# Three rounded products for the routing layer of a fused attention and slot-routing kernel

## The reference

```
x = x + attention(layernorm(x))
x = x + routing(layernorm(x))

attention: a charge q = tanh(x Wc + bc) and a normalised vector shell = x Ws + bs,
           features phi = W_combine (powers of q) x (cos, sin of shell omega + bias),
           causal softmax of phi phi^T * decay, times values x Wv, times W_out
routing:   h = gelu([x, slot_mean] w1^T + b1)      # 512 -> 128, slot_mean is the same for all tokens
           logits = (h w2^T + b2) / (|tau| + 0.1)  # 64 slots
           alpha = softmax over the 8 largest logits, 0 elsewhere
           slots gather x by alpha, pass a GRU cell, are spread again by alpha, and wo
```

## Time and profile before

| | us |
|---|---|
| median of 3 runs | 731.66 (730.02 to 732.78) |
| the profiled execution's own time | 732.47 |
| its span | 730.6 |
| PE busy | 713.6 (98%) |
| DVE busy | 591.7 (81%) |
| ACT busy | 429.0 (59%) |
| POOL busy | 388.4 (53%) |
| mean granted clock of TensorE | 0.994 |

### The profile page before, as it was taken

One profiled execution on the slowest core, in us unless ns is written; L12 is line 12 of the kernel. 1 busy time (PEld: TensorE's weight loads), 2 busy tenths in 40 slices (PEclk: granted clock), 3 DMA queues, 4 the chain that ended last, 5 costly groups with the idle time before them and its releaser, 6 DMA issues.

```text
span 730.6 us, 14749 instructions
## 1 busy us (share of the span) xinstructions
PE 713.6 (98%) x4528; PEld 546.6 (75%) x4528; DVE 591.7 (81%) x1833; ACT 429.0 (59%) x841; POOL 388.4 (53%) x828
## 2 busy tenths in 40 slices
PE   8989999999899999999999999999999999999996
PEld 5866877786686977778697777779687777866774
DVE  6888777788779888897978889797888889786755
ACT  4457576638356485665648575555757565565351
POOL 5545676354645558284655738365573837544300
PEclk9999999999999999999999999999999999999999
DMA  8252020203332140323224042322304132121005
GB/s 258 77 168 59 1 59 2 58 0 90 86 116 59 54 120 2 116 59 116 59 64 110 2 129 45 116 58 87 88 2 144 31 116 59 58 59 59 1 6 168
DMA packets 49110, 54.11 MB, mean 74 GB/s; under 512 B 6215, under 2 KB 40585, under 8 KB 49033
## 3 DMA queue, kind: packets, MB, share of 16 engines
q1 hardware_dynamic: 48258, 52.64, 26.0%
q10 hardware_dynamic: 774, 0.53, 0.2%
HBM read 20.65 MB, written 16.78 MB: 51 GB/s over the span
## 4 chain that ended last, share of the span: by engine, by line
PE 92%; DVE 2%; DMA 2%; issue 1%; SPq 1%; ACT 1%; POOL 0%; DVEq 0%; POOLq 0%
PE ps L435 19%; PE ps L314 17%; PE ps L340 16%; PE ps L461 8%; PE ps L406 6%; PE ps L510 5%; PE ps L574 4%; PE ps L495 4%; PE ps L385 4%; PE ps L473 2%; PE ps L554 2%; PE ps L387 2%; DMA VS<-in_W_scT 1%; PE ps L588 1%; DMA xmT<-Z 1%
## 5 line engine op out<-in xcount | busy, mean ns | idle before, releaser
L435 PE MATMUL ps<-VS,ET 128*128 128x257 f32 x640 | 159.3, 383 | 0.3 <-ACT ET L765 0.2
L435 PEld LDWEIGHTS ps<-VS,ET 128*128 128x128 f32 x640 | 112.6, 190 | 23.8 <-issue 11.9
L251 POOL TENSOR_TENSOR Z<-Z,QB 128x512 f32<-128x512 f32 x60 | 76.5, 1275 | 93.2 <-ACT Z L746 91.5
L704 ACT ACTIVATE xn<-X,rs 128x256 f32<-128x256 f32 x128 | 66.3, 593 | 54.2 <-POOL rs L1303 54.2
L755 ACT ACTIVATE E<-ps,nmax 128x128 f32<-128x128 f32 (+3 forms) x128 | 63.8, 527 | 47.7 <-DVE nmax L967 47.5
L898 DVE TENSOR_TENSOR VS<-ps,biasM 128x354 f32<-128x354 f32 x128 | 66.8, 525 | 30.0 <-PE ps L340 27.6
L765 ACT ACTIVATE ET<-ps 128x128 f32<-128x128 f32 (+3 forms) x128 | 55.0, 431 | 59.2 <-PE ps L314 58.9
L340 PE MATMUL ps<-W1h,xh 128*128 128x354 f32 x256 | 87.2, 341 | 0.4 <-DVE xl L885 0.2
L340 PE MATMUL ps<-W1l,xh 128*128 128x354 f32 x256 | 83.3, 326 | 0.0
L340 PE MATMUL ps<-W1h,xl 128*128 128x354 f32 x256 | 82.7, 323 | 0.0
L243 POOL TENSOR_TENSOR tg<-VS 128x256 f32<-128x256 f32 x30 | 18.5, 619 | 94.9 <-DVE VS L898 85.0
(11 more groups left out here) (203 smaller groups left out, 1602.9 us busy)
## 6 DMA issues: line engine op xcount, KB each, us to landing
X<-in_x SPq DMA_DIRECT2D x32, 512.0 KB, 4.5
xmT<-Z SPq DMA_DIRECT2D x120, 128.0 KB, 2.3
out_x<-X SPq DMA_DIRECT2D x30, 512.0 KB, 3.2
out_x<-X SPq DMA_DIRECT2D x4, 256.0 KB, 2.3
X<-in_gru_whhT SPq DMA_DIRECT2D x1, 768.0 KB
wih<-in_gru_wihT SPq DMA_DIRECT2D x1, 768.0 KB
X<-in_W_v ACTq DMA_DIRECT2D x1, 256.0 KB, 4.5
X<-in_W_outT ACTq DMA_DIRECT2D x1, 256.0 KB, 6.8
```

The costliest lines, as they stand in the source:

```text
L251: e.tensor_tensor(Z[:, i + 1, :], Z[:, i, :], QB[:, :], ALU.mult).then_inc(s["zm"], 1)
L435: ins = e.matmul(p[:, 0:D + 1], ET[:, r % 2, j * 128:j * 128 + 128], VS[:, (2 * k + d) % 4, j, 0:D + 1], start=j == 0, stop=j == i)
L704: ins = e.activation(xn[:, d, t, :], X[:, b % NX, t, :], ACT.Identity, bias=rs[:, d, 2, t:t + 1], scale=rs[:, d, 1, t:t + 1])
```

## The change

- hidden makes six rounded products in place of two float32 ones: w1h x high part, w1h x low part, w1l x high part, for each half of the channels.
- xm_copy writes xmT rounded, as the high part. A new DVE step xm_low(k, d, c) writes the low part xmL = bank - xmT and counts the new semaphore xml; hidden and the next user of the T bank wait for xml in place of xmT.
- slot_setup makes w1h and w1l of w1a once (two more DVE instructions; SLOTS becomes 14).
- The written order of all five programs is new, in the first list, the loop and the last list. Shown below for the loop.

```diff
+        xmL = sb("xmL", [128, 2, 2, N], FR)
+        w1h = sb("w1h", [128, 2, H], FR)
+        w1l = sb("w1l", [128, 2, H], FR)
...
-        SETUP, SOFT, CHAIN, SLOTS = 6, 10, 5, 12
+        SETUP, SOFT, CHAIN, SLOTS = 6, 10, 5, 14
...
             def xm_t(k, d, c):
                 b = 2 * k + d
-                p, before = T.take(s["xmT"], 2 * b + c + 1)
+                p, before = T.take(s["xml"], 2 * b + c + 1)
...
-                e.wait_ge(s["xmT"], 2 * b + 2)
+                e.wait_ge(s["xml"], 2 * b + 2)
                 if b == 0:
                     e.wait_ge(s["slot_evac"], SLOTS)
-                for c in range(2):
-                    ins = e.matmul(p[:, :], w1a[:, c, :], xmT[:, d, c, :], start=c == 0, stop=c == 1)
+                parts = [(w, x, c) for c in range(2)
+                         for w, x in ((w1h, xmT.bitcast(FR)), (w1h, xmL), (w1l, xmT.bitcast(FR)))]
+                for j, (w, x, c) in enumerate(parts):
+                    ins = e.matmul(p[:, :], w[:, c, :], x[:, d, c, :], start=j == 0, stop=j == 5)
                 ins.then_inc(s["h_mm"], 1)
...
-                e.activation(xmT[:, d, c, :], at["xm", b, c][:, :], ACT.Copy).then_inc(s["xmT"], 1)
+                e.activation(xmT[:, d, c, :].bitcast(FR), at["xm", b, c][:, :], ACT.Copy).then_inc(s["xmT"], 1)
...
+            @live
+            def xm_low(k, d, c):
+                b = 2 * k + d
+                e.wait_ge(s["xmT"], 2 * b + c + 1)
+                if k:
+                    e.wait_ge(s["h_mm"], 2 * (k - 1) + d + 1)
+                e.tensor_tensor(xmL[:, d, c, :], at["xm", b, c][:, :], xmT[:, d, c, :],
+                                ALU.subtract).then_inc(s["xml"], 1)
...
+                e.tensor_copy(w1h[:, :, :], w1a[:, :, :]).then_inc(s["slot_evac"], 1)
+                e.wait_ge(s["slot_evac"], SLOTS - 2)
+                e.tensor_tensor(w1l[:, :, :], w1a[:, :, :], w1h[:, :, :].bitcast(FP), ALU.subtract).then_inc(s["slot_evac"], 1)
```

PE's first list, where the first attention begins, and its loop and last list:

```diff
-            proj(1, 1, 0); z_t(0); proj(1, 1, 1); proj(1, 1, 2); phi(0); proj(1, 1, 3); logits(0, 0)
-            e_t(0, 0); e_t(0, 1); q_t(1); logits(0, 1); xn_t(2, 0, 0); e_t(0, 2); e_t(0, 3); values(0, 0)
+            proj(1, 1, 0); z_t(0); proj(1, 1, 1); phi(0); proj(1, 1, 2); logits(0, 0); proj(1, 1, 3)
+            e_t(0, 0); values(0, 0); e_t(0, 1); q_t(1); logits(0, 1); e_t(0, 2); xn_t(2, 0, 0); values(0, 1)
...
-                xn_t(p, 0, 0); xn_t(p, 0, 1); e_t(n, 0); gx_rz(m); proj(p, 0, 0); proj(p, 0, 1)
-                proj(p, 0, 2); proj(p, 0, 3); xn_t(p, 1, 0); values(n, 0); xn_t(p, 1, 1); gx_n(m)
-                xm_t(f, 0, 0); xm_t(f, 0, 1); out_mm(g, 1); logits(n, 1); proj(p, 1, 0); proj(p, 1, 1)
-                proj(p, 1, 2); proj(p, 1, 3); e_t(n, 1); xm_t(f, 1, 0); e_t(n, 2); xm_t(f, 1, 1)
-                values(n, 1); e_t(n, 3); hidden(f, 0); q_t(p); hidden(f, 1); e_t(n, 4); values(n, 2)
-                logits(n, 2); route(f); values(n, 3); z_t(p); e_t(n, 5); rt_t(f); values(n, 4); values(n, 5)
-                e_t(n, 6); slot_v(m); e_t(n, 7); values(n, 6); al_t(m); values(n, 7); phi(p); gather(f)
+                xn_t(p, 0, 0); xn_t(p, 0, 1); gx_rz(m); e_t(n, 0); proj(p, 0, 0); proj(p, 0, 1)
+                proj(p, 0, 2); proj(p, 0, 3); xn_t(p, 1, 0); gx_n(m); values(n, 0); xn_t(p, 1, 1)
+                xm_t(f, 0, 0); xm_t(f, 0, 1); logits(n, 1); out_mm(g, 1); proj(p, 1, 0); proj(p, 1, 1)
+                proj(p, 1, 2); proj(p, 1, 3); e_t(n, 1); e_t(n, 2); xm_t(f, 1, 0); xm_t(f, 1, 1)
+                values(n, 1); e_t(n, 3); hidden(f, 0); hidden(f, 1); q_t(p); values(n, 2); e_t(n, 4)
+                logits(n, 2); route(f); values(n, 3); e_t(n, 5); z_t(p); rt_t(f); values(n, 4); al_t(m)
+                values(n, 5); e_t(n, 6); slot_v(m); e_t(n, 7); values(n, 6); values(n, 7); phi(p); gather(f)
                 logits(p, 0); out_mm(m, 0); gi_t(f)
...
-            gx_rz(y); xm_t(z, 0, 0); xm_t(z, 0, 1)
+            xm_t(z, 0, 0); xm_t(z, 0, 1); gx_rz(y); xm_t(z, 1, 0); xm_t(z, 1, 1)
             e.wait_ge(s["E"], 8 * NP)
             warm(3)
-            hidden(z, 0); xm_t(z, 1, 0); xm_t(z, 1, 1); gx_n(y)
-            hidden(z, 1)
+            hidden(z, 0); hidden(z, 1)
+            gx_n(y)
             warm(4)
             route(z); al_t(y); rt_t(z); out_mm(x, 1)
             warm(21)
```

The middle of DVE's loop, where xm_low comes in:

```diff
-                row_max(n, 3); vs(p, 0, 0); vs(p, 0, 1); vs(p, 0, 2); vs(p, 0, 3); attended(n, 0)
-                xn_low(p, 1, 0); xn_low(p, 1, 1); candidate(m); finish(g, 1, 0); row_max(n, 4)
-                finish(g, 1, 1); vs(p, 1, 0); vs(p, 1, 1); row_max(n, 5); vs(p, 1, 2); vs(p, 1, 3)
-                norm_sum(p, 0); lm_stats(n, 0); norm_sum(p, 1); attended(n, 1); new_slots(m); lm_stats(n, 1)
-                phase(p); turns(p); unwind(p); clamp(p); attended(n, 2); row_max(n, 6); lm_stats(n, 2)
+                xn_low(p, 0, 1); finish(g, 0, 1); row_max(n, 3); gates(m); vs(p, 0, 0); vs(p, 0, 1)
+                vs(p, 0, 2); vs(p, 0, 3); xn_low(p, 1, 0); candidate(m); attended(n, 0); xn_low(p, 1, 1)
+                xm_low(f, 0, 0); xm_low(f, 0, 1); finish(g, 1, 0); finish(g, 1, 1); vs(p, 1, 0)
+                norm_sum(p, 0); row_max(n, 4); vs(p, 1, 1); vs(p, 1, 2); vs(p, 1, 3); lm_stats(n, 0)
+                norm_sum(p, 1); xm_low(f, 1, 0); xm_low(f, 1, 1); row_max(n, 5); attended(n, 1); phase(p)
+                turns(p); unwind(p); clamp(p); attended(n, 2); lm_stats(n, 1); new_slots(m); lm_stats(n, 2)
```

```diff
-            load_x(0); load_x(1); weight_loads(); load_x(2); first_loads(); load_x(3); slot_loads()
-            load_x(4); load_x(5); load_x(6); load_x(7); load_x(8); load_x(9); z_moves(1); z_moves(2)
+            load_x(0); weight_loads(); load_x(1); load_x(2); first_loads(); load_x(3); slot_loads()
+            load_x(4); load_x(5); load_x(6); load_x(7); load_x(8); z_moves(1); load_x(9); z_moves(2)
+            z_moves(3); store(0, 0)
             for it in range(3, NP - 1):
-                f, o = it, it - 3
-                z_moves(f); store(o, 0); store(o, 1); load_x(2 * it + 4); load_x(2 * it + 5)
+                n, g, o = it + 1, it - 2, it - 3
+                store(o, 1); load_x(2 * it + 4); load_x(2 * it + 5); z_moves(n); store(g, 0)
```

## The result

The changed kernel takes 727.26 us, the median of six runs (725.11 to 730.84), against 731.88 for the kernel before on the same chip: ratio 0.9944, 95% interval 0.9917 to 0.9970. In a later job it took 726.67 against 733.29: 0.9908 [0.9884, 0.9932]. So it is faster by 4.6 us in the first job and 6.6 in the later one, 46% and 65% of what was forecast (10.1 off the 731.66).

A forecast was written before the change was run, and what follows sets the result against it. PE was taken to bound the kernel, busy through every pass: 732.47 - 10.1 (products) + 1.5 (VectorE) - 1.5 (start) + 0 (tail) = 722.4 us, or 721.6 on the median's scale; range 717 to 729.

The forecast's parts named there:

- the first e_t's wait: Before the loop: PE's 1.59 us idle and slow clock behind it would shrink, with proj(1, 1, 3) put ahead of e_t.
- rival 2: In the loop: VectorE hand-offs lose 0.3 to 0.5 us per pair, half the gain eaten, 727 us; chance 0.19.
- Saved, 10.1 us: Hidden layer on PE: six rounded products replace 1.72 us by 1.36, 32 times, less 17 switches of 0.08 us.
- the upper bound, 0.232: Hidden's product rate if overhead grows in proportion to columns: 0.233 us for 512, saving 8.9 us; 0.227 was taken.
- VectorE's hand-offs, +1.5: In the loop: 64 xm_low subtractions on tight margins make PE lose 0.1 us a pair, 1.5 us in all.
- Before the loop, -1.5: Start-up: less idle and slow clock before the first e_t, against added setup; between -4.0 and +0.7, taken as -1.5 us.
- three pairs' -1.6: The start's share of the per-pair forecast: three pairs at 0.54 us each, 0.63 saved and 0.09 lost.
- the W_scT wait: Before the loop: PE's 0.8 us wait for W_scT, now issued before the second batch of x, might go.
- The tail, 0: Last list: one switch saved against a 0.68 us subtraction in each chain; taken as 0, between -1 and +2 us.
- Rival 1: VectorE becomes the bound, xm_low delaying evacuations for PE's three banks; slower, 740 us with half exposed; chance 0.10.

The follow-up runs named there:

- order_only: The new lists with the old float32 hidden products and no subtractions, against the kernel before: 732.10 us, ratio 1.0007.
- four_exp: The changed kernel without hidden's w1l products and with Exp in place of Gelu: 724.27 us, 0.9892 of the kernel before, pass 41.75.
- x_first: The changed kernel with the second batch of x loaded ahead of the weight loads again: 726.11 us, 0.9912 of the kernel before.
- tail_sv: The changed kernel with slot_values(x) moved before attended(z, 7) in VectorE's last list: 724.30 us, 0.9900 of the kernel before.
- products_only: The kernel before with its old lists, the rounded products and their subtractions put in: 740.64 us, ratio 1.0112.
- light2: four_exp with VectorE's lm_stats(n, 1) and lm_stats(n, 2) moved behind attended(n, 5) in the loop: 719.25 us, pass 41.36.

## Why the prediction was right and wrong

The direction was right, and so were parts of the mechanism: PE was the bound, hidden's records start 0.23 us apart, the wait for xml is 0.07 us in after's passes, DVE is at 37.4 of a pass (forecast 38.4), the first e_t's wait fell from 1.59 us to 0.5 (its values wait 0.5 more) and the clock over 50 to 60 us rose to 1.00. The saving was not: 4.6 us for 10.1, and the time was off by 5.7 us. What failed is the price of the new lists outside the loop: the tail, taken as 0, cost +2.6 us, and the start, taken as -1.5 beside its three pairs, gave 1.1 us less than forecast in one profile and 4.9 less in the other. The term for VectorE in the loop was near in size, with another cause. That rival 2 had the measured 727 is luck: it put the loss into hand-offs in every pass, 0.3 to 0.5 us a pair, where 0.15 was lost. By the steps:

- *Saved, 10.1 us.* PE gives 0.60 us a pass against 0.63 forecast, over 16 pairs 9.6. Hidden itself gives 0.52: the rate was at the upper bound, 0.232, and 0.07 is the wait for the last subtraction. The 0.08 at the e_t ahead, which I had not counted, made up for most of it.
- *VectorE's hand-offs, +1.5.* The size for the loop is near: 0.15 us a pass lost, some 0.06 more than taken. The path was wrong. I walked xm_low to hidden and to the bank of finish; the first loses 0.07, and without any subtraction the pass is the same 41.74. What was missing is that DVE's list behind the last bias add runs without a pause to the banks of e_t(n, 7) and values(n, 6), just as long in order_only without a subtraction, where PE's 42.2 hid it. A share of busy time (35.9 of 42.2) does not show such a stretch. It also caps what further cuts on PE can bring: four_exp took 0.59 us off what lies ahead on PE (0.47 and 0.12) and got none of it.
- *Before the loop, -1.5 with the three pairs' -1.6.* Measured +1.8 and -2.0 in two profiles. The e_t idle and its clock went as said; the W_scT wait, which I expected to go or to shrink from 0.8 us, was 1.24 in the slower profile and is not listed in the other; and I priced the later x at nothing. In the slower profile there are new gaps at 9 to 18 us and two stretches at the 1.2 GHz level; that the late x made them is read from these traces and x_first's, not shown by the medians.
- *The tail, 0.* This failed most clearly: +2.6 by order_only against before, over the +2 I had as its upper bound. I looked at transposes and finish and not at slot_values, moved behind the one operation that waits for PE's last values; moved back in tail_sv, it gives 1.5.
- *Rival 1* (VectorE the bound) had 0.10. Its mechanism is what products_only shows, at +9.2 us and in lists that were not the change's.

Still open: 1.1 us of the tail; how much of the start is chance and how much the load order, since I have one trace of each kernel but after; and whether light2's edit, which took 0.39 us off four_exp's pass, does so in after, where it was tried only along with the e_t move that undid it.

## What to carry to other kernels

A pass with PE busy for all of it can stand on a second bound just as long: follow the chain from the last bias add through every engine back to PE before pricing a cut on PE, and look at what the next engine waits for if its own work in that chain shrinks (here POOL's power, which made 1.3 us of subtractions free). When an in-order list is rewritten, ask of each moved entry what it now stands behind; here one entry in the tail cost 1.5 us of a forecast gain of 10, and in the slower profile, with a load moved back, PE stood short of work and the clock fell.

## What the runs showed of the hardware

The rounded products cost in proportion to columns, 0.161 us at 354 and 0.232 at 512, 9% over one column a cycle at 2.4 GHz at both sizes, with no fixed part that these two could tell. A change to Gelu's table and back took ScalarE 1.28 us each in a pass. And TensorE's clock is not settled by what the program does alone: behind the same waits in the tail, with PE busy 1.50 of 3 us in both, the granted clock of the next 3 us was 0.50 in one execution (x_first) and 1.00 in another (after).
